# A fused attention and mixture-of-experts layer: GpSimd's indirect DMAs in groups that wait for TensorE

## The chip, the cores and the metric

The kernel runs on one core of a Trainium2 chip. The metric is the device time of one execution in microseconds (us); lower is better. It is given as the median of several runs.

## The reference

One transformer layer on x of 16 sequences x 128 tokens x 256 features (2048 tokens), in float32, with a context of the same shape:

```python
x = x + xattn(layernorm(x), ctx, ctx, pad_mask, subsq_mask, Wq, bq, Wk, bk, Wv, bv)   # 16 heads of 16
h = layernorm(x)
ys = geglu(h @ Ws1 + bs1) @ Ws2 + bs2                      # shared expert, hidden width 512
logits = (h @ Wr + br) / 1.5
top_val, top_idx = top_k(logits, 2); top_w = softmax(top_val)
yE = geglu(h @ We1[e] + be1[e]) @ We2[e] + be2[e]          # 12 experts, hidden width 768
x = x + ys + sum over the two chosen e of top_w * yE
```

`geglu(a|g)` is `a * gelu(g)`. The reference computes every expert for every token and weights with zeros; the kernel computes only the chosen ones, 128 token copies at a time.

## The kernel before, in words

Each engine has its own program and they meet at semaphores. TensorE multiplies float32r operands split in a high and a low part, so each product takes three matmuls.

**Attention.** The sequences go in eight pairs p = 0..7 (`each_pair`; `PAIRS` is 8). Pairs 1 to 4 are a loop, pairs 0, 5, 6 and 7 are written out. Each pair has four units n = 0..3 (a sequence and half of its heads). In unit n TensorE computes `scores` (L540, L545, then `scores_ready` +1, so it is 4p+n+1 after unit n), transposes the probabilities of the unit before (L557, `pt_ready`), multiplies them with the values (L569, `pv_done`), and every second unit transposes the output back (L578). Between these it works for the next pair: transposes and projections (L461, L484, L492), and the router of the pair before (L461, L509). ScalarE copies the transposes out of PSUM (L832 `probT`, L837 `outT`, which waits for `pv_done`) and takes exponentials (L841); VectorE finds maxima (L1090), subtracts them (L1096), divides and adds the residual. Pair 7 has no next pair, so its units have less in them.

**Routing.** VectorE chooses the two experts of each token in three batches of 8, 4 and 4 tiles of 128 tokens (`BATCHES`) and writes row numbers (`idx_top`, `rows_ready` +1 each). GpSimd then scatters the normalized tokens with `scatter(t)` (L1523 to L1527): two indirect DMAs of 128 rows x 1 KB for tile t, from SBUF (`xn2_all`) to DRAM (`rows_in`). In GpSimd's program these stand at four places:
- pair 6, behind its layernorm step for pair 5 (`rstd`, L1425 and L1427) and waits for `rows_ready` 1: tiles 0 to 3, 8 DMAs;
- pair 7: tiles 4 to 7, then, behind `rows_ready` 2, tiles 8 to 11, in all 16 DMAs;
- after `expert(0)`, behind `rows_ready` 3: tiles 12 to 15, 8 DMAs.

Then `load_up_bias(0)` (L1533, waits for `out_rows_ready`), `expert(1)` and so on. `expert(e)` splits the weights that were loaded to `stage1` and `stage2` into the ring: `convert` (L1433, L1437), the next load (L1492), `convert_down` (L1446, L1450), the next load (L1496). SyncE loads the first rows of a slot only when all 32 scatters have landed (`scattered`, L428).

**Feed forward.** TensorE goes through 8 tiles of the shared expert (`FRONT` = 8), 43 slots of routed tokens (`SLOTS`), and the other 8 tiles of the shared expert (`BACK` = 8; `B0` = 51 is the number of tiles before them). A tile is: up product (L657, `up_ready`), bias on VectorE (L1313), gelu on ScalarE (L899), gate on VectorE (L1318), transposes (L671, `ht_ready`), high part on ScalarE (L906), low part on VectorE (L1322), down product (L704, L708 for a slot, L706 to L708 for a shared tile, ending in L710 with `y_ready`). The next tile's tokens are transposed in L688 (`xt_ready`) and split in L916 and L1327. VectorE adds the result to `x_all` (L1340, shared tile) or writes `y_row` (L1337, slot); both add 1 to `y_done`, which is therefore B0+1 when the first back tile is done. SyncE stores the slots' results to DRAM (`rows_out`, L432).

**The end.** When `y_done` has reached FRONT + SLOTS and all stores of slots have landed, GpSimd gathers every token's two results with 32 indirect DMAs of 128 rows x 1 KB (L1601, two for each of 16 tiles). VectorE adds them (L1403, `combine(t)`): tiles 2(i-2) and 2(i-2)+1 after back tile i, for i = 2 to 7, and tiles 12 to 15 after the last back tile. SyncE stores each finished tile (L451).

Of the kernel before, what the change touches and what calls it, by code (L numbers as in the profile page):

```python
# [28 lines left out]
TILES = N // P  # L29
# [22 lines left out]
def build(nc, x_d, ctx_d, pad_d, sub_d, wq_d, wk_d, wv_d, bq_d, bk_d, bias_d, tab_d, ws1_d, ws2_d, w1_d,  # L52
# [177 lines left out]
    def sem(name):  # L230
# [11 lines left out]
    scores_ready, shifted, maxed, exp_done, pt_ready, pt_copied, pv_done, normed = map(sem, (  # L242
        "scores_ready", "shifted", "maxed", "exp_done", "pt_ready", "pt_copied", "pv_done", "normed"))
# [27 lines left out]
    y_ready, y_done, shared_bias_in, sel_down_ready = map(sem, (  # L271
        "y_ready", "y_done", "shared_bias_in", "sel_down_ready"))
# [70 lines left out]
    B0 = FRONT + SLOTS  # L343
# [6 lines left out]
    with block:  # L350
# [1071 lines left out]
        def _(gp):  # L1422
            def rstd(var_sem, out_sem, mv, ve_t, rs_t, q, step_sem):
                gp.wait_ge(var_sem, q + 1)
                pool.tensor_tensor(ve_t[:, :], mv[:, :, 1], eps[:, :], ALU.add).then_inc(step_sem, 1)  # L1425
                gp.wait_ge(step_sem, q + 1)
                pool.tensor_tensor(rs_t[:, :], ve_t[:, :], half[:, :], ALU.pow).then_inc(out_sem, 1)  # L1427

            def convert(src, hi_ap, lo_ap, count):

                n = src.shape[1]
                for c in range(0, n, PIECE):
                    last = pool.tensor_scalar(hi_ap[:, c:c + PIECE], src[:, c:c + PIECE], 1.0, 0.0, ALU.mult, ALU.add)  # L1433
                last.then_inc(conv_hi, 1)
                gp.wait_ge(conv_hi, count)
                for c in range(0, n, PIECE):
                    last = pool.tensor_tensor(lo_ap[:, c:c + PIECE], src[:, c:c + PIECE],  # L1437
                                              hi_ap[:, c:c + PIECE].bitcast(f32), ALU.subtract)
                return last

            def convert_down(src, both_ap, count):

                both = both_ap.rearrange("p (c h n) -> p c h n", h=2, n=D)
                raw = src.rearrange("p (c n) -> p c n", n=D)
                for c in range(0, raw.shape[1], 2):
                    last = pool.tensor_scalar(both[:, c:c + 2, 0, :], raw[:, c:c + 2, :], 1.0, 0.0, ALU.mult, ALU.add)  # L1446
                last.then_inc(conv_hi, 1)
                gp.wait_ge(conv_hi, count)
                for c in range(0, raw.shape[1], 2):
                    last = pool.tensor_tensor(both[:, c:c + 2, 1, :], raw[:, c:c + 2, :],  # L1450
                                              both[:, c:c + 2, 0, :].bitcast(f32), ALU.subtract)
                return last
# [6 lines left out]
            for c in range(KC):  # L1459
                n = H  # L1460
# [30 lines left out]
            def load_raw1(e):  # L1491
                gp.dma_start(stage1[:, :].rearrange("p (c n) -> p c n", c=KC),  # L1492
                             w1_d[e, :, :].rearrange("(c p) n -> p c n", p=P)).then_inc(raw1_in, 16)

            def load_raw2(e):
                gp.dma_start(stage2[:, :].rearrange("p (c n) -> p c n", n=D),  # L1496
                             w2_d[e, :, :].rearrange("(c p) n -> p c n", p=P)).then_inc(raw2_in, 16)
# [6 lines left out]
            def pair(p, par, first, last):  # L1504
                if not first:
                    rstd(ln2_var, ln2_rs, mv2, ve2, rs2, p - 1, pstep2)
                if not last and not (isinstance(p, int) and p + 2 >= PAIRS):
                    rstd(ln1_var, ln1_rs, mv1, ve1, rs1, p + 2, pstep)
                if isinstance(p, int) and p == PAIRS - 2:
                    gp.wait_ge(zero_out, 16 * FILLS)  # L1510
                    gp.wait_ge(xn2_saved, 16 * 4)
                    gp.wait_ge(rows_ready, 1)
                    for t in range(0, 4):
                        scatter(t)
                if last:
                    for t in range(4, 8):
                        scatter(t)
                    gp.wait_ge(xn2_saved, 16 * 6)
                    gp.wait_ge(rows_ready, 2)
                    for t in range(8, 12):  # L1520
                        scatter(t)

            def scatter(t):  # L1523
                for k in range(2):
                    gp.indirect_dma_start(
                        out=rows_in, out_offset=bass.IndirectOffsetOnAxis(ap=idx_top[:, k, t:t + 1], axis=0),
                        in_=xn2_all[:, t * D:(t + 1) * D], in_offset=None).then_inc(scattered, 16)  # L1527

            each_pair(gp, pair)
            rstd(ln2_var, ln2_rs, mv2, ve2, rs2, PAIRS - 1, pstep2)  # L1530

            def load_up_bias(e):
                gp.dma_start(up_bias[:, e % RING, :],  # L1533
                             bias_d[e, 0:2 * HR].partition_broadcast(P))\
                    .then_inc(up_bias_in if e else first_bias_in, 16)

            def expert(e):

                r = e % RING
                if e > 0:  # L1540
                    load_up_bias(e)
                gp.wait_ge(raw1_in, 16 * (e + 1))
                convert(stage1[:, :], ring[:, r, 0:W1R], ring[:, r, W1R:2 * W1R], 2 * e + 3).then_inc(pconv, 1)
                gp.wait_ge(pconv, e + 1)
                if e + 1 < E:
                    load_raw1(e + 1)
                else:
                    gp.dma_start(stage1[:, 0:W1S].rearrange("p (c n) -> p c n", c=KC),
                                 ws1_d.rearrange("(c p) n -> p c n", p=P)).then_inc(raw1_in, 16)
                gp.wait_ge(raw2_in, 16 * (e + 1))  # L1550
                if e > 0:
                    gp.wait_ge(up_bias_in, 16 * e)
                convert_down(stage2[:, :], ring[:, r, 2 * W1R:], 2 * e + 4)\
                    .then_inc(converted, 1)
                gp.wait_ge(converted, e + 2)
                if e + 1 < E:
                    load_raw2(e + 1)
                else:
                    gp.dma_start(stage2[:, 0:W2S].rearrange("p (c n) -> p c n", n=D),
                                 ws2_d.rearrange("(c p) n -> p c n", p=P)).then_inc(raw2_in, 16)  # L1560
# [3 lines left out]
            gp.wait_ge(normed, B)  # L1564
            gp.wait_ge(xb_free, PAIR_STEPS_END + 2)
            expert(0)

            gp.wait_ge(xn2_saved, 16 * PAIRS)
            gp.wait_ge(rows_ready, len(BATCHES))
            for t in range(12, TILES):  # L1570
                scatter(t)
            gp.wait_ge(tables_ready, 1)
            gp.wait_ge(out_rows_ready, 1)
            load_up_bias(0)
            expert(1)
            for e in range(2, E):
                if e == 2:
                    gp.wait_ge(y_done, FRONT)
                else:
                    done = gp.value_load(tab_cum[0:1, e - RING:e - RING + 1], min_val=1, max_val=SLOTS + FRONT)  # L1580
                    gp.wait_ge(y_done, done)
                    pool.tensor_tensor(ptick[:, :], half[:, 0:1], half[:, 0:1], ALU.add)
                expert(e)
# [13 lines left out]
            for par in range(2):  # L1597
                gp.wait_ge(y_out[par], 16 * ((SLOTS + 1 - par) // 2))
            for t in range(TILES):
                for k in range(2):  # L1600
                    gp.indirect_dma_start(  # L1601
                        out=gath[:, t, k, :], out_offset=None, in_=rows_out,
                        in_offset=bass.IndirectOffsetOnAxis(ap=idx_out[:, k, t:t + 1], axis=0))\
                        .then_inc(gathered[t], 16)
# [59 lines left out]
```

## Time and profile before

| | |
|---|---|
| median of 3 runs | 753.22 us (750.91 to 760.72) |
| the profiled execution's own time | 759.51 us |
| its span, first to last instruction | 757.7 us |
| mean granted TensorE clock | 0.920 of full |
| TensorE matmuls busy | 646.5 us (85%) |
| VectorE busy | 484.7 us (64%) |
| GpSimd busy | 347.5 us (46%) |
| ScalarE busy | 300.7 us (40%) |

Times are from the span's start. In the trace PE is TensorE, DVE is VectorE, ACT is ScalarE, POOL is GpSimd, SP is SyncE. A row of a timeline gives start, duration, engine, line, operation, what is written from what, how often; in brackets stands how long the engine had been idle before and what ended that. "remote" there is an end for which the trace has a semaphore update, but no instruction that had just finished; "issue" is an end without such an update at that moment. PEclk is the clock that TensorE was granted, of 2.4 GHz; its two levels are 2.4 and 1.2 GHz.

### The profile page before, as it was taken

To read this page: it belongs to the slowest core of one execution; us is meant where nothing else is said; L and a number is where in the kernel's file an instruction comes from. 1 tells how busy PE (TensorE), PEld (TensorE's weight loads), DVE (VectorE), ACT (ScalarE), POOL (GpSimd) and SP (SyncE) were. 2 spreads that over 40 slices of the span, in tenths; PEclk is the share of its full clock that TensorE was granted. 3 is DMA by queue.
4 is the path that set the end of the run, shared out by engine and by line. 5 is a ranking of instruction groups with operands and counts; after the bars stand their busy time and mean duration, and the time that the engine had idled before them with its cause. 6 is when DMAs were issued, how large, how long until landed. Compare 5 with 4: busy or idle time off the path is not lost.

```text
span 757.7 us, 14868 instructions
## 1 busy us (share of the span) xinstructions
PE 646.5 (85%) x4276; PEld 536.5 (71%) x4277; DVE 484.7 (64%) x1077; ACT 300.7 (40%) x685; POOL 347.5 (46%) x404
## 2 busy tenths in 40 slices
PE   7889989998968287699999999999999999993264
PEld 6778777877755265587878878787887878883163
DVE  7667767768734237976666767676666666762086
ACT  4445555554532042135434444444444444430021
POOL 3950000000120707796497489478974860027500
PEclk9989999999965668999999999999999999996687
DMA  9964522536010300553443544353545320113311
GB/s 294 402 218 163 210 107 101 208 140 251 24 47 1 117 8 17 177 181 114 153 166 119 193 148 167 123 193 133 194 129 177 121 78 28 35 42 119 90 42 56
DMA packets 48178, 100.07 MB, mean 132 GB/s; under 512 B 4624, under 2 KB 23824, under 8 KB 48144
## 3 DMA queue, kind: packets, MB, share of 16 engines
q1 hardware_dynamic: 36320, 51.06, 19.0%
q0 software_dynamic: 11120, 48.24, 19.0%
q10 hardware_dynamic: 704, 0.33, 0.2%
q8 instruction: 20, 0.33, 0.2%
q14 instruction: 14, 0.11, 0.0%
HBM read 58.19 MB, written 39.19 MB: 129 GB/s over the span
## 4 chain that ended last, share of the span: by engine, by line
PE 72%; DVE 10%; issue 7%; another core or an unknown queue 5%; ACT 5%; POOL 1%; DMA 1%; DVEq 0%; ACTq 0%; SPq 0%; POOLq 0%
PE ps_s L657 27%; PE ps_o L704 8%; PE ps_o L708 5%; PE ps_t L557 4%; PE ps_o L569 4%; PE ps_s L545 4%; PE ps_t L671 3%; PE ps_t L484 2%; ACT probT L832 2%; PE ps_x L484 2%; PE ps_s L540 2%; DVE x_all L1403 2%; PE ps_x L679 1%; PE ps_s L671 1%
## 5 line engine op out<-in xcount | busy, mean ns | idle before, releaser
L657 PE MATMUL ps_s<-ring,xTh 128*128 (+1 forms) x644 | 193.0, 422 | 13.2 <-issue 12.6
L657 PEld LDWEIGHTS ps_s<-ring,xTh 128*128 128x128 f32 x644 | 112.1, 192 | 31.4 <-issue 13.5
L1313 DVE TENSOR_TENSOR ag<-ps_s,up_bias 128x512 f32<-128x512 f32 x145 | 99.9, 689 | 26.3 <-remote 14.4
L657 PE MATMUL ps_s<-ring,xTl 128*128 (+1 forms) x322 | 101.6, 397 | 0.0
L1437 POOL TENSOR_TENSOR ring<-stage,ring 128x512 fp32r<-128x512 f32 x80 | 100.6, 1291 | 1.2
L1425 POOL TENSOR_TENSOR ve<-mv,eps 128x2 f32<-128x2 f32 x16 | 3.9, 247 | 207.2 <-DVE mv L1122 166.0
L704 PE MATMUL ps_o<-ring,hTh 128*128 x258 | 95.9, 409 | 1.0 <-DVE hTl L1322 1.0
L708 PE MATMUL ps_o<-ring,hTl 128*128 (+1 forms) x322 | 92.5, 287 | 0.0
L906 ACT ACTIVATE hTh<-ps_t 128x256 fp32r<-128x256 f32 x118 | 45.2, 384 | 109.8 <-PE ps_t L671 80.1
L899 ACT ACTIVATE ps_s<-ag 128x256 f32<-128x256 f32 x161 | 62.6, 389 | 48.8 <-DVE ag L1313 45.2
L1318 DVE TENSOR_TENSOR ag<-ag,ps_s 128x256 f32<-128x256 f32 x161 | 67.7, 421 | 20.2 <-ACT ps_s L899 2.1
L832 ACT ACTIVATE probT<-ps_t 128x512 f32<-128x512 f32 x64 | 38.2, 596 | 87.0 <-PE ps_t L557 83.3
L657 PEld LDWEIGHTS ps_s<-ring,xTl 128*128 128x128 f32 x322 | 61.3, 190 | 14.3
L1322 DVE TENSOR_TENSOR hTl<-ps_t,hTh 128x256 fp32r<-128x256 f32 x118 | 49.5, 420 | 26.3 <-ACT hTh L906 21.3
L708 PEld LDWEIGHTS ps_o<-ring,hTl 128*128 128x128 f32 x322 | 63.2, 196 | 0.0
L1601 POOL DMA_INDIRECT gath<-rows_out,idx_out x32 | 30.6, 957 | 67.1 <-DMA rows_out<-y_row 57.7
L704 PEld LDWEIGHTS ps_o<-ring,hTh 128*128 128x128 f32 x258 | 48.5, 188 | 11.0 <-issue 1.5
L1337 DVE TENSOR_TENSOR y_row<-ps_o,y_lo 128x256 f32<-128x256 f32 x43 | 18.3, 425 | 55.8 <-ACT y_lo L924 55.8
L671 PE MATMUL ps_t<-const,ag 128*128 128x128 f32 x236 | 46.7, 280 | 5.9 <-issue 5.8
L1450 POOL TENSOR_TENSOR ring<-stage,ring 128x512 fp32r<-128x512 f32 x40 | 50.6, 1292 | 1.2
L557 PE MATMUL ps_t<-const,prob 128*128 128x128 f32 x256 | 45.3, 304 | 6.6 <-ACT probT L832 5.2
L1433 POOL TENSOR_SCALAR ring<-stage 128x512 fp32r<-128x512 f32 x80 | 47.2, 618 | 4.7 <-DVE logits L1037 4.3
(253 smaller groups left out, 1275.1 us busy)
## 6 DMA issues: line engine op xcount, KB each, us to landing
rows_in<-y_row SPq DMA_DIRECT2D x8, 3328.0 KB, 11.2
stage<-in_w POOLq DMA_DIRECT2D x12, 1536.0 KB, 6.7
stage<-in_w POOLq DMA_DIRECT2D x12, 768.0 KB
up_bias<-in_bias POOLq DMA_DIRECT2D x12, 768.0 KB, 4.6
xrow<-rows_in SPq DMA_DIRECT2D x43, 128.0 KB, 2.3
rows_out<-y_row SPq DMA_DIRECT2D x43, 128.0 KB, 1.7
cbuf<-in_ctx SPq DMA_DIRECT2D x8, 256.0 KB, 3.2
xn_all<-xn2p SPq DMA_DIRECT2D x8, 256.0 KB
```

Of the source, the lines that this page charges most:

```text
L557: last = pe_.transpose(ps_t[:, 0, g * P:(g + 1) * P], prob[n % 2][:, jj, g, :], ident)
L657: last = pe_.matmul(ps_s[:, i, :], x[:, c, :], weights(place, off + c * full + i * 2 * D, 2 * D), start=n == 0, stop=n == 5)
L671: last = pe_.transpose(hid_bank[i][:, c * P:(c + 1) * P], ag[i][:, 0, c * P:(c + 1) * P], ident)
L704: pe_.matmul(ps_o[:, :], hTh[i][:, c, :], weights(place, a, 2 * D), start=first, stop=False)
L708: pe_.matmul(ps_o[:, 0:D], hTl[i][:, c, :], weights(place, a, D), start=False, stop=False)
L832: act.activation(probT[:, jj, :, :], ps_t[:, 0, :].rearrange("p (g t) -> p g t", g=4), ACT.Identity).then_inc(pt_copied, 1)
L899: act.activation(ps_s[:, i, D:2 * D], ag[i][:, 1, :], ACT.Gelu).then_inc(gelu_done[i], 1)
L1313: vec.tensor_tensor(ag[i][:, :, :].rearrange("p a n -> p (a n)"), ps_s[:, i, :], bias, ALU.add)\
L1318: vec.tensor_tensor(ag[i][:, 0, :], ag[i][:, 0, :], ps_s[:, i, D:2 * D], ALU.mult).then_inc(hid_done[i], 1)
L1322: vec.tensor_tensor(hTl[i][:, :, :], hid_bank[i].rearrange("p (c n) -> p c n", c=2), hTh[i][:, :, :].bitcast(f32), ALU.subtract).then_inc( ...
L1437: last = pool.tensor_tensor(lo_ap[:, c:c + PIECE], src[:, c:c + PIECE], hi_ap[:, c:c + PIECE].bitcast(f32), ALU.subtract)
L1450: last = pool.tensor_tensor(both[:, c:c + 2, 1, :], raw[:, c:c + 2, :], both[:, c:c + 2, 0, :].bitcast(f32), ALU.subtract)
```

## The change

In GpSimd's program the scatters and gathers get waits between them:
- pair 6: before tiles 0, 1, 2 and 3 a wait for the scores of unit 0, 1, 2 and 3 of that pair;
- pair 7: tiles 4 and 5 wait for the scores of unit 0, tiles 6 and 7 for those of unit 1, tiles 8 and 9 (beside their old waits) for those of unit 3;
- tiles 10 and 11 go out inside `expert(0)`, between the load for expert 1 that follows `convert` and `convert_down`;
- tiles 12 and 13 keep their place, tiles 14 and 15 wait for `y_done` 3;
- the gathers of tiles 4 and 5 wait for `y_done` B0+1, and so on to those of tiles 14 and 15, which wait for B0+6.

The number of DMAs and their sizes stay the same.

```diff
@@ pair() of gpsimd, p = PAIRS - 2, and the last pair
-                    for t in range(0, 4):
-                        scatter(t)
+                    for n in range(4):
+                        gp.wait_ge(scores_ready, 4 * p + n + 1)
+                        scatter(n)
                 if last:
-                    for t in range(4, 8):
-                        scatter(t)
+                    for n in range(2):
+                        gp.wait_ge(scores_ready, 4 * p + n + 1)
+                        scatter(4 + 2 * n)
+                        scatter(5 + 2 * n)
                     gp.wait_ge(xn2_saved, 16 * 6)
                     gp.wait_ge(rows_ready, 2)
-                    for t in range(8, 12):
+                    gp.wait_ge(scores_ready, 4 * p + 4)
+                    for t in (8, 9):
                         scatter(t)
@@ expert(e), after the load of stage1 for the next expert
+                if e == 0:
+                    for t in (10, 11):
+                        scatter(t)
                 gp.wait_ge(raw2_in, 16 * (e + 1))
@@ after expert(0)
-            for t in range(12, TILES):
+            for t in (12, 13):
+                scatter(t)
+            gp.wait_ge(y_done, 3)
+            for t in (14, 15):
                 scatter(t)
@@ the gathers
             for t in range(TILES):
+                if t % 2 == 0 and t >= 4:
+                    gp.wait_ge(y_done, B0 + t // 2 - 1)
                 for k in range(2):
```

## Rows read from the trace of the kernel before

**Rows 1.** The page, part 2: granted TensorE clock in 40 slices.

```profile
PEclk9989999999965668999999999999999999996687
```

**Rows 2.** The page, part 4: the chain that ended last, by engine.

```profile
PE 72%; DVE 10%; issue 7%; another core or an unknown queue 5%; ACT 5%; POOL 1%; DMA 1%; DVEq 0%; ACTq 0%; SPq 0%; POOLq 0%
```

**Rows 3.** Instructions by line: the scatters, then the gathers (ns min/median/max, starts in us).

```profile
L1525 POOL DMA_INDIRECT rows_in<-xn_all,idx_top x32: 956/960/1210, 205.2 to 318.5; - x32
...
L1601 POOL DMA_INDIRECT gath<-rows_out,idx_out x32: 942/946/1171, 675.7 to 714.9; - x32
```

**Rows 4.** Timeline around the first eight scatters (pair 6).

```profile
205.22 1.21 POOL L1525 DMA_INDIRECT rows_in<-xn_all,idx_top  x1 [0.20 <-issue]
...
208.91 0.60 ACT L832 ACTIVATE probT<-ps_t 128x512 f32<-128x512 f32 x1 [0.15 <-PE ps_t L557]
...
210.13 1.07 PE L569 MATMUL ps_o<-probT,v_sb 128*32 128x128 f32 x16
...
214.33 0.96 POOL L1525 DMA_INDIRECT rows_in<-xn_all,idx_top  x1 [0.30 <-issue]
216.90 0.60 ACT L837 ACTIVATE outT<-ps_o 128x512 f32<-128x512 f32 x1 [7.39 <-remote]
```

**Rows 5.** Timeline around the next sixteen scatters (pair 7).

```profile
245.44 1.17 POOL L1525 DMA_INDIRECT rows_in<-xn_all,idx_top  x1 [0.19 <-issue]
...
254.10 1.90 PE L569 MATMUL ps_o<-probT,v_sb 128*32 128x128 f32 x16 [3.16 <-ACT probT L832]
254.49 0.96 POOL L1525 DMA_INDIRECT rows_in<-xn_all,idx_top  x1 [0.30 <-issue]
...
264.61 0.96 POOL L1525 DMA_INDIRECT rows_in<-xn_all,idx_top  x1 [0.30 <-issue]
265.52 0.60 ACT L837 ACTIVATE outT<-ps_o 128x512 f32<-128x512 f32 x1 [11.47 <-remote]
```

**Rows 6.** Timeline of the gathers and the back tiles.

```profile
683.19 0.62 PE L657 MATMUL ps_s<-ring,xTl 128*128 128x512 f32 x2
...
685.10 0.42 DVE L1340 TENSOR_TENSOR x_all<-ps_o,x_all 128x256 f32<-128x256 f32 x1 [3.06 <-remote]
...
692.92 0.69 DVE L1313 TENSOR_TENSOR ag<-ps_s,up_bias 128x512 f32<-128x512 f32 x1 [4.98 <-remote]
...
694.85 0.95 POOL L1601 DMA_INDIRECT gath<-rows_out,idx_out  x1 [0.30 <-issue]
...
698.90 0.63 PE L671 MATMUL ps_t<-const,ag 128*128 128x128 f32 x2
...
712.10 2.08 PE L657 MATMUL ps_s<-ring,xTh 128*128 128x512 f32 x4 [12.57 <-issue]
...
721.07 0.42 DVE L1340 TENSOR_TENSOR x_all<-ps_o,x_all 128x256 f32<-128x256 f32 x1 [8.70 <-remote]
...
751.07 0.42 DVE L1340 TENSOR_TENSOR x_all<-ps_o,x_all 128x256 f32<-128x256 f32 x1 [2.71 <-PE ps_o L710]
```

**Rows 7.** TensorE timeline: starts of the mask products (L540) of four units.

```profile
191.09 0.60 PE L540 MATMUL ps_s<-mask_b,ident_b 128*128 128x512 bf16 x2
...
205.07 0.61 PE L540 MATMUL ps_s<-mask_b,ident_b 128*128 128x512 bf16 x2
...
218.46 1.06 PE L540 MATMUL ps_s<-mask_b,ident_b 128*128 128x512 bf16 x2
...
245.95 1.03 PE L540 MATMUL ps_s<-mask_b,ident_b 128*128 128x512 bf16 x2
```

**Rows 8.** Busy time by window: PE, PEld, DVE, ACT, POOL, PEclk, DMA share, GB/s.

```profile
217.50:244.30 26.80, 23.10 (x140) 17.71 (x142) 13.70 (x31) 9.09 (x15) 0.05 (x1) 0.56 0.00 1
...
724.90:751.10 26.20, 22.07 (x121) 18.85 (x121) 20.45 (x47) 6.72 (x19) 0.00 (x0) 0.89 0.12 41
```

**Rows 9.** GpSimd's timeline behind the last eight scatters.

```profile
322.07 1.15 POOL L1533 DMA_DIRECT2D up_bias<-in_bias  x2 [2.58 <-DVE idx_out L1253]
...
349.03 0.56 POOL L1533 DMA_DIRECT2D up_bias<-in_bias  x1 [6.62 <-DVE x_all L1340]
```

## The prediction

> **What bounds the kernel now.** I read the clock by slices first [rows 1]: it is near full nearly everywhere, and falls to 0.5 to 0.8 in two places, slices 12 to 16 (208 to 303 us) and the last four (682 us to the end). The chain of waits [rows 2] is TensorE's for 72%, but has 7% "issue" and 5% of an unknown releaser, together about 90 us of 757.7. The instructions by line [rows 3] show what those places have in common: the 32 scatters run between 205.2 and 319.5 us and the 32 gathers between 675.7 and 715.9 us. Each takes 0.96 us of GpSimd, and one starts every 1.26 us (the first scatter of pair 6 at 205.22, the eighth at 214.33 [rows 4]).
>
> The timeline says what happens in such a burst. In pair 6 TensorE ends its value product at 211.20, and ScalarE's copy, which waits for nothing else, starts at 216.90, marked "remote": the semaphore update is there, but 5.7 us after the matmul [rows 4]. The last scatter had ended at 215.29. In pair 7 the value product ends at 256.00 and the same copy starts at 265.52; the sixteenth scatter runs 264.61 to 265.57 [rows 5]. In the gathers an up product ends at 683.81 and VectorE's bias step for it starts at 692.92; TensorE starts its next up product only at 712.10, after 12.57 us of idleness; and the down product finished by 699.1 lets VectorE go at 721.07 [rows 6]. So my reading is: **TensorE's releases are held up while GpSimd issues indirect DMAs one after the other**, and they get through when it stops. At a burst's start it does no harm: ScalarE took the release of a product that ended 3.5 us into the first burst after 0.15 us [rows 4]. Releases 6 us in and later are the ones held.
>
> How soon after a burst's end they get through differs: 1.6 us in pair 6 (215.29 to 216.90), none in pair 7, 5.2 us in the gathers (715.9 to 721.07). I take 1.6 us and keep 0 and 5.2 as ends.
>
> **Pair 6.** GpSimd reaches tile 0 at 205.22 because of its layernorm step, when the scores of units 0 and 1 are long done; those of unit 2 begin at 205.07 [rows 7] and are done before tile 2's turn at 210.3. So three of the four waits pass at once, six DMAs go unbroken, to 212.8, and the last two wait for unit 3's scores. The held release then comes at 212.8 + 1.6 = 214.4 instead of 216.9: gain 2.5 us (ends 4.1 and 0). The wait needs TensorE to go on, and TensorE waits for nothing of GpSimd's there; behind it in GpSimd's queue stands the layernorm step of pair 6, some 25 us later. The last two DMAs are 2.5 us long, below the 3.5 us that did no harm: 0.
>
> **Pair 7.** The layernorm step again brings GpSimd there after the scores of unit 1 have begun, so tiles 4 to 7 are eight DMAs unbroken, 245.44 to 255.45 [rows 5]. Then it waits for unit 3's scores, which need the held release. That comes at 255.45 + 1.6 but not before the product ends at 256.00, so about 257.5 instead of 265.5: gain 8.0 us (ends 9.5 and 4.8). Tiles 8 and 9 follow as four DMAs of 5.0 us where there were none; a release in their last 1.5 us may be late: -0.5 us (0 to -5.0, the group's length).
>
> **Tiles 10 to 15.** Four DMAs (5.0 us) enter `expert(0)` ahead of the second conversion, so both the expert's weights and the last eight scatters are up to 5.0 us later. VectorE writes its tables during the last burst and GpSimd idles 2.58 us behind it until `out_rows_ready` [rows 9]; 2.4 us of delay are left, and GpSimd idles 6.62 us before expert 2 for `y_done` [rows 9], so the conversions absorb it. SyncE's first row loads wait for all scatters and come some 5 us later too, at about 327; their tokens are used beside the eighth front tile, which ends by 349 [rows 9]. `y_done` 3 has come when tiles 14 and 15 are reached. What remains is held releases in the front tiles: -1 us (0 to -5).
>
> **Gathers.** `y_done` B0+2 comes at 685.5 [rows 6] and B0+1 a tile before it, both before they are asked for. So 16 gathers go unbroken as now, to 695.8, and only the wait for B0+3 holds. Releases open at 695.8 + 1.6 = 697.4; TensorE's down product ends at about 699.5 anyway [rows 6], and its next input, split by ScalarE and VectorE after the release, is ready by then. So `y_done` B0+3 comes at about 700 instead of 721.5. From there to the last back tile it takes 30.0 us now (721.07 to 751.07, five tiles of 6.0 us [rows 6], clock 0.89 [rows 8]). I add 2 us because the clock will be low for longer at its start, and four groups of gathers, 5.0 us each beside a tile of 6.0 us. A release in a group's last 1.5 us may be late; 0.75 us each, 3 us. The last tile then ends at 700 + 30 + 5 = 735 instead of 751.5: gain 16.5 us. Best end: without these 5 us 21.5, and 3.3 more if the clock is 1 and not 0.89 over the 30 us: 24.8. Worst: the release 5.2 us late instead of 1.6 and each group holding its tile for its whole 5.0 us: 16.5 + 3 - 3.6 - 20 = -4. The last gathers wait for B0+6, two tiles (12 us) before they are needed, and take 5 us: they don't set the end.
>
> **Sum.** 2.5 + 8.0 - 0.5 - 1 + 16.5 = 25.5 us against the profiled execution's 759.51: 734.0. That execution lies 6.3 us above the median of 753.22, and the runs spread over 9.8 us. If that spread is in the held releases, it goes with them and 734.0 stands; if it lies elsewhere, 727.7. I take the middle, 731, in round numbers **730 us**, and move all prices below by the same -4.
>
> **The clock.** After the first stall TensorE ran 26.8 us at a mean of 0.56, busy for 23.1 of them [rows 8]; before it, at full clock, two units took 14.0 us [rows 7], and after it the three from 218.46 to 245.95 took 27.5 instead of 21.0. So a stall costs up to 6.5 us more behind its end. I give nothing of that back, since six DMAs in a row still leave a stall of about 3 us at the same place. The Trainium skill's TensorE: Matmul & The Clock Gate ("HAM oscillation") says that idle gaps drop the clock, so that they are paid twice; by that rule the shorter gap would give back up to these 6.5 us as well. The trace agrees that the low level follows the gap; whether a gap half as long spares it, no row shows.
>
> **Rivals.**
> - **A, the stalls go with their aftermath.** All best ends: 4.1 + 6.5 (clock) + 9.5 + 24.8 = 44.9 us, so 714.6, moved 711. For it: a release 3.5 us into a burst was on time. Against: pieces of 6, 8 and 16 DMAs stay unbroken. 0.15.
> - **B, paced gathers are a burst all the same.** A group is 5.0 us of a 6.0 us tile, so GpSimd hardly pauses, and what holds releases may not clear in 1 us. Then the gather term is 0 and 9.0 us are left: 750.5, moved 747. For it: 5.2 us passed after the last gather before anything came through. Against: each group starts only after a release has come. 0.13.
> - **C, slower: each gather group meets its tile's releases.** The group is now let go by `y_done`, just as the next tile's up products start, so every tile from B0+4 on has its releases inside a group. The trace has one release 9.1 us late (692.92 for the product of 683.81 [rows 6]). With 9.1 us on each of five tiles the last ends at 700 + 5 x 15.1 = 775.5, 24 us later than now; less 9 us of the scatters, 774.5, moved 771. It decides from tiles of (751.5 + 9 - 700) / 5 = 12.1 us on. Against: the start of a burst did no harm. 0.06.
> - **D, the releases aren't held by GpSimd's DMAs.** Most waits pass at once, the total stays: 753. For it: the last eight scatters, 309 to 319 us, sit beside no such drop of the clock [rows 1]. Against: both other scatter bursts and the gathers do. 0.06.
>
> My forecast has 0.60, with its own range of 720 to 741. The range for 8 times in 10 reaches to A and B: 710 to 748. About 2%, 15 us, can be told from no change, so below 738.2 counts as faster: most of my case and A, 0.78; the rest of it, B and D, 0.16; C, 0.06.
>
> **What would show it.** In pair 6 six scatters, a gap, two; in pair 7 eight, a gap, four. ScalarE's `outT` copies start near 214 and 257 us. In the gathers 16 without a break to 695.8, then four at a time, VectorE's third back tile (L1340) near 700, then tiles of 6 to 7 us, no "remote" or "issue" idleness over 3 us. Conversions from expert 2 on unchanged against `y_done`. I am wrong if the held releases come as late as before though GpSimd has stopped, if GpSimd's four-DMA groups each show one, or if the scatters in pair 6 have gaps where I let them pass.

## The result, and the profile after

The kernel after takes 730.00 us (median of 6 runs, 727.31 to 732.60), the kernel before 756.34 us (median of 6, 750.35 to 760.72): ratio 0.966 (0.959 to 0.972), 26.3 us faster. The forecast was 730. The profiled execution took 727.32 us. A ratio here and below leaves out executions more than 1.5% above the fastest of the same kernel, so that it can differ a little from the quotient of the two medians.

The page after: the span, the busy times, the clock by slices and the chain's shares.

```profile
span 725.4 us, 14869 instructions
...
PE 639.4 (88%) x4276; PEld 532.0 (73%) x4277; DVE 485.3 (67%) x1077; ACT 301.3 (42%) x685; POOL 347.7 (48%) x404
...
PEclk9989999999988678899999999999999999999697
...
PE 75%; DVE 11%; issue 7%; ACT 4%; another core or an unknown queue 1%; DMA 1%; POOL 1%; SPq 0%; DVEq 0%; ACTq 0%; POOLq 0%
```

Against [rows 1 and 2]: "an unknown releaser" went from 5% to 1% of the chain, the clock dips are shallower, and the engines are as busy as before. So the time came out of waiting.

The timeline after, scatters of pairs 6 and 7 with ScalarE's copies of the value products between them:

```profile
204.96 1.15 POOL L1529 DMA_INDIRECT rows_in<-xn_all,idx_top  x1 [0.26 <-issue]
...
211.50 0.96 POOL L1529 DMA_INDIRECT rows_in<-xn_all,idx_top  x1 [0.30 <-issue]
213.76 0.60 ACT L837 ACTIVATE outT<-ps_o 128x512 f32<-128x512 f32 x1 [4.56 <-remote]
...
218.57 0.96 POOL L1529 DMA_INDIRECT rows_in<-xn_all,idx_top  x1 [6.11 <-PE ps_s L545]
...
238.76 1.16 POOL L1529 DMA_INDIRECT rows_in<-xn_all,idx_top  x1 [0.20 <-issue]
...
247.42 0.60 ACT L837 ACTIVATE outT<-ps_o 128x512 f32<-128x512 f32 x1 [4.17 <-remote]
247.81 0.96 POOL L1529 DMA_INDIRECT rows_in<-xn_all,idx_top  x1 [0.30 <-issue]
...
252.77 0.96 POOL L1529 DMA_INDIRECT rows_in<-xn_all,idx_top  x1 [3.99 <-PE ps_s L545]
```

Six scatters, a gap, two; then eight, a gap, four: the groups are those forecast. The first late release comes 8.80 us after the first scatter (11.68 in [rows 4]), the second 8.66 us after it (20.08 in [rows 5]). The second comes before the eighth scatter starts, so a burst does not have to end for a release to get through.

The timeline after, gathers and back tiles:

```profile
661.87 1.05 POOL L1613 DMA_INDIRECT gath<-rows_out,idx_out  x1 [57.57 <-DMA rows_out<-y_row]
...
680.74 0.95 POOL L1613 DMA_INDIRECT gath<-rows_out,idx_out  x1 [0.30 <-issue]
682.55 0.38 ACT L906 ACTIVATE hTh<-ps_t 128x256 fp32r<-128x256 f32 x1 [10.20 <-remote]
...
683.49 0.55 PE L706 MATMUL ps_o<-ring,hTh 128*128 128x256 f32 x1 [11.72 <-issue]
...
684.76 0.38 ACT L916 ACTIVATE xTh<-ps_x 128x256 fp32r<-128x256 f32 x1 [1.55 <-remote]
...
686.64 0.42 DVE L1340 TENSOR_TENSOR x_all<-ps_o,x_all 128x256 f32<-128x256 f32 x1 [0.37 <-PE ps_o L710]
...
687.33 0.94 POOL L1613 DMA_INDIRECT gath<-rows_out,idx_out  x1 [5.65 <-DVE x_all L1340]
...
693.79 0.94 POOL L1613 DMA_INDIRECT gath<-rows_out,idx_out  x1 [1.76 <-DVE x_all L1340]
...
698.49 0.28 PE L710 MATMUL ps_o<-bias_tab,sel_s 128*128 128x256 f32 x1
...
699.52 0.42 DVE L1340 TENSOR_TENSOR x_all<-ps_o,x_all 128x256 f32<-128x256 f32 x1 [0.62 <-PE ps_o L710]
...
718.78 0.42 DVE L1340 TENSOR_TENSOR x_all<-ps_o,x_all 128x256 f32<-128x256 f32 x1 [3.25 <-PE ps_o L710]
```

Sixteen gathers still go unbroken (661.87 to 681.69) and still hold TensorE: it stands idle for 11.72 us before 683.49, because ScalarE's `hTh` is released only at 682.55, 0.9 us after the burst. Then four groups of four follow, 1.7 us apart, with a back tile every 6.4 us, and not one "remote" among them. Yet their releases are not on time: TensorE's product ends at 698.77 and VectorE takes it at 699.52, 0.75 us later and 1.05 us after the group's last gather, and it is 0.75 to 0.78 us in each of the four groups.

Stage by stage, gain of the profiled executions (757.7 against 725.4 us of span) beside the forecast:

| stretch | before | after | gain | forecast |
|---|---|---|---|---|
| first scatter to late `outT`, pair 6 | 205.22 to 216.90 | 204.96 to 213.76 | 2.9 | 2.5 |
| to pair 7's first scatter | to 245.44 | to 238.76 | 3.5 | 0 |
| to late `outT`, pair 7 | to 265.52 | to 247.42 | 11.4 | 8.0 |
| to the first front tile's end (L1340) | to 297.93 | to 280.21 | -0.4 | -0.5 |
| to the first gather | to 675.74 | to 661.87 | -3.8 | -1 |
| first gather to the span's end | to 757.7 | to 725.4 | 18.4 | 16.5 |
| up to the first scatter | 205.22 | 204.96 | 0.3 | 0 |
| sum | | | 32.3 | 25.5 |

On the medians it is 26.3.

### The profile page after: what moved, and what is told of

The parts are those of the page before. It is cut to its first block, busy times and chain, and to the rows that moved or that the text cites. A ratio compares the mean times of both kernels' runs of the same rounds, so it can differ in the third digit from the quotient of the medians.

```text
span 725.4 us, 14869 instructions
## 1 busy us (share of the span) xinstructions
PE 639.4 (88%) x4276; PEld 532.0 (73%) x4277; DVE 485.3 (67%) x1077; ACT 301.3 (42%) x685; POOL 347.7 (48%) x404
## 4 chain that ended last, share of the span: by engine, by line
PE 75%; DVE 11%; issue 7%; ACT 4%; another core or an unknown queue 1%; DMA 1%; POOL 1%; SPq 0%; DVEq 0%; ACTq 0%; POOLq 0%
PE ps_s L657 29%; PE ps_o L704 8%; PE ps_o L708 5%; PE ps_t L557 4%; PE ps_o L569 4%; PE ps_s L545 4%; PE ps_t L671 3%; PE ps_x L484 2%; PE ps_t L484 2%; DVE x_all L1403 2%; ACT probT L832 2%; PE ps_s L540 2%; PE ps_o L706 2%; PE ps_o L710 1%; PE ps_x L679 1%
## 5 line engine op out<-in xcount | busy, mean ns | idle before, releaser
L1337 DVE TENSOR_TENSOR y_row<-ps_o,y_lo 128x256 f32<-128x256 f32 x43 | 18.3, 425 | 55.7 <-ACT y_lo L924 55.7
L706 PE MATMUL ps_o<-ring,hTh 128*128 128x256 f32 x64 | 21.7, 339 | 31.3 <-issue 27.9
```

## The experiments

Theory H: while GpSimd issues indirect DMAs without a pause, TensorE's releases to other engines are held, and a pause lets them through. Rival D: the late releases have another cause, and the waits gain by ordering alone. Beside these, each part of the change was priced alone.

The runs fell into four sittings, on chips 8, 12, 1 and 9, each with its own runs of the kernel before. That kernel took 754 and 759 us (medians) on chips 12 and 9, much as in the result, but 697 us on chips 8 and 1. Each verdict below is against the kernel before of the same sitting.

**Sitting 1 (chip 8, kernel before 697.10 us, 25 runs, one of them of 1535.75 us): the parts alone.**

`gathers_only` is the kernel before with the waits of the gathers:

```diff
                 for t in range(TILES):
+                    if t % 2 == 0 and t >= 4:
+                        gp.wait_ge(y_done, B0 + t // 2 - 1)
```

> The kernel before with only the waits between the gathers. Theory (TensorE's releases are held while GpSimd issues indirect DMAs without a break): the scatter bursts keep their held releases, ScalarE's outT copies near 216.9 and 265 us, and the gather stage is shorter by 16 to 19 us, as in the changed kernel: some 18 us under the time of before, about 738. Rival (the gathers gain only because the scatters left the engines in another state): under 8 us gained.

Measured 697.34 us (10 runs), ratio 1.001 (0.997 to 1.004).

`scatters_only` is the kernel after without these two lines:

> The changed kernel without the waits between the gathers. Theory: the scatter part is worth what the profiles differ by at the first gather, 13.9 us, so about 742; the gather stage keeps its three long waits and its 82 us from first gather to end. Rival (the two parts overlap in what they save): under 8 us gained.

Measured 700.71 us (10), ratio 1.005 (1.003 to 1.008).

`landing_waits` leaves the scatters alone and has the gathers pause every four DMAs for something that has nothing to do with TensorE, the landing of the last ones:

```diff
                 for t in range(TILES):
+                    if t % 2 == 0 and t >= 2:
+                        gp.wait_ge(gathered[t - 1], 32)
```

> The kernel before, where each group of four gathers waits until the group before has landed, with no wait for TensorE at all. Theory (a pause of GpSimd is what lets releases through, whoever it waits for): pauses of about 1 to 2 us after every 4 gathers, no wait of over 3 us for an unknown releaser in the back tiles, gain 18 to 28 us (more than gathers_only, as no 16 go unbroken), about 730. Rival (the wait for TensorE is what matters, since it starts each group when no release is due): held releases as before in most groups, gain under 8 us.

Measured 710.22 us (4), ratio 1.022 (1.014 to 1.030).

`ten_behind` is the kernel after with tiles 10 and 11 moved back out of `expert(0)`:

```diff
-                if e == 0:
-                    for t in (10, 11):
-                        scatter(t)
...
-            for t in (12, 13):
+            for t in (10, 11, 12, 13):
                 scatter(t)
```

> The changed kernel with the scatters of tiles 10 and 11 moved out of expert(0), to just before those of tiles 12 and 13. Theory (they push GpSimd's second conversion onto VectorE's short row number operations, which then take 1 us each, and cost most of the 4.2 us that the front tiles lost against before): front tiles 2 to 4 us shorter, 727 or less. Rival (the loss comes from scatters beside the front tiles, wherever they stand): twelve scatters nearly in a row there, no gain or a loss of up to 3 us.

Measured 699.63 us (10), ratio 1.002 (0.997 to 1.007).

None of the times expected could be met, since here there was nothing to win; what `ten_behind` expected of the front tiles is taken up below. The timeline of `gathers_only`, whose scatters are those of the kernel before, shows ScalarE's copies in pairs 6 and 7 beside the first and last of pair 7's sixteen scatters, then one product and its use in the back tiles:

```profile
210.28 0.60 ACT L837 ACTIVATE outT<-ps_o 128x512 f32<-128x512 f32 x1 [1.87 <-PE ps_o L569]
...
231.69 1.17 POOL L1525 DMA_INDIRECT rows_in<-xn_all,idx_top  x1 [0.19 <-issue]
...
237.95 0.60 ACT L837 ACTIVATE outT<-ps_o 128x512 f32<-128x512 f32 x1 [1.76 <-PE ps_o L569]
...
248.30 0.60 ACT L837 ACTIVATE outT<-ps_o 128x512 f32<-128x512 f32 x1 [1.19 <-PE ps_o L569]
...
251.06 0.96 POOL L1525 DMA_INDIRECT rows_in<-xn_all,idx_top  x1 [0.31 <-issue]
...
668.03 0.28 PE L710 MATMUL ps_o<-bias_tab,sel_s 128*128 128x256 f32 x1
...
668.36 0.42 DVE L1340 TENSOR_TENSOR x_all<-ps_o,x_all 128x256 f32<-128x256 f32 x1
```

Sixteen scatters without a break, 0.96 us each, every 1.26 us, as in [rows 5]. Two copies start 6.3 and 16.6 us into them, each 0.07 us after TensorE's product. In the back tiles VectorE takes the product 0.05 us after its end (668.31), with gathers going out all the while. No wait of TensorE, ScalarE or VectorE around the scatters or gathers ends "remote", in this or any other kernel profiled in such a sitting, and the back tiles come every 5.7 us. So the bursts are the same in both kinds of sitting, and what differs is whether they hold releases. The difference of the two kernels before is 57 to 63 us. From the end of the first front tile to the first gather both kinds take 377.8 us (266.94 to 644.74 here, 297.93 to 675.74 before); all of the difference lies in the stages with the bursts. So it is the price of the held releases with their aftermath, and about what there is to win by removing them.

**Sitting 2 (chip 12, kernel before 753.97 us, 7 runs): both kernels once more,** to see whether result and trace belong together.

> The kernel before, unchanged, profiled on the chip of this call. In the last call its median was 697 us, not 756, and the scatter bursts of gathers_only and landing_waits held no release. Theory now: held releases belong to some chips or cores and not to others, and they are the whole difference of about 58 us. So either the median is near 697 and the profile shows no wait of over 3 us for an unknown releaser in the bursts, or it is near 756 and shows those of the first profile. Rival (the 697 us came from something else, say a faster clock in the routed tiles): near 697 with held releases still in the bursts, and the time gained evenly over the span.

> The changed kernel, unchanged, beside it. Theory: where before takes about 697 us the waits have nothing to remove and cost what the front tiles lose, 0 to 5 us: 697 to 703. Where before takes about 756 it is near 730 again. Rival (the waits gain by something beside held releases): over 5 us faster than before on a chip without them.

The kernel after took 730.24 us (4), ratio 0.969 (0.960 to 0.977). The profiled execution of the kernel before took 760.49 us and has its late copies back:

```profile
216.32 0.60 ACT L837 ACTIVATE outT<-ps_o 128x512 f32<-128x512 f32 x1 [7.37 <-remote]
...
264.29 0.60 ACT L837 ACTIVATE outT<-ps_o 128x512 f32<-128x512 f32 x1 [13.60 <-issue]
...
717.69 0.69 DVE L1313 TENSOR_TENSOR ag<-ps_s,up_bias 128x512 f32<-128x512 f32 x1 [14.93 <-remote]
```

The gain goes with the held releases: where they are there it is 24 and 26 us, where they aren't its parts are worth nothing. (The kernel after as a whole was never timed there.)

**Sitting 3 (chip 1, kernel before 696.76 us, 19 runs).** `paced` applies the finding that six or eight DMAs are still too long a group. Pairs 6 and 7 scatter in groups of four behind the scores of units 1 and 3, tiles 10 to 15 go out behind `expert(0)` (two waits for `y_done` 3 stand between them, both long met), and every group of four gathers waits for the latest tile. Against the kernel after, in part:

```diff
-                    for n in range(4):
-                        gp.wait_ge(scores_ready, 4 * p + n + 1)
-                        scatter(n)
+                    for n in range(2):
+                        gp.wait_ge(scores_ready, 4 * p + 2 + 2 * n)
+                        scatter(2 * n)
+                        scatter(2 * n + 1)
...
-                    gp.wait_ge(scores_ready, 4 * p + 4)
+                    gp.wait_ge(pv_done, 2 * UNITS - 2)
                     for t in (8, 9):
...
-                if t % 2 == 0 and t >= 4:
-                    gp.wait_ge(y_done, B0 + t // 2 - 1)
+                if t % 2 == 0 and t >= 2:
+                    gp.wait_ge(y_done, B0 + t // 2)
```

> The changed kernel with groups of four from the start: gathers of tiles 2 and 3 wait for the first back tile, those of 14 and 15 for the seventh; in pairs 6 and 7 four scatters, then a wait for unit 3's scores, four more, and the last four of pair 7 wait for the value products; tiles 10 and 11 after expert(0). Theory (no group of four holds a release): where before takes about 756 the outT waits and the 10 us waits of the first 16 gathers go too, 15 to 25 us under the changed kernel, 705 to 715. Rival (four in a row already hold when the group is let go by TensorE): 725 or more. Where before takes about 697: 695 to 705.

Measured 699.94 us (10), ratio 1.003 (1.000 to 1.006).

`gathers_only` and `landing_waits` were run again:

> The same kernel as gathers_only, for a chip on which before takes about 756 us. Theory (holds of releases in each unbroken burst, the two parts add up): outT copies late by 6 and 9 us or more in the scatter bursts as in before, gather stage (first gather to end) 63 to 66 us instead of 82, so 735 to 740. Rival (the parts aren't independent): gather stage over 72 us. If before takes about 697 here: no difference, as in the first call.

> The same kernel as landing_waits, for a chip on which before takes about 756 us: each group of four gathers waits for the landing of the group before, not for TensorE. Theory (GpSimd's pause lets releases through): pauses of 2 to 3 us, no wait for an unknown releaser over 3 us in the back tiles; the gather stage is as short as in gathers_only_2 or up to 5 us shorter. Rival (the wait must be tied to TensorE's progress): such waits in most groups, stage over 72 us. If before takes about 697 here: some 13 us slower than before, as in the first call.

They took 698.94 us (10), ratio 1.000 (0.996 to 1.004), and 710.38 us (4), ratio 1.016 (1.010 to 1.021).

`direct_pool` was to tell an indirect DMA from a plain one, by issuing the gathers of the kernel before as plain DMAs of the same size:

```diff
-                    gp.indirect_dma_start(
-                        out=gath[:, t, k, :], out_offset=None, in_=rows_out,
-                        in_offset=bass.IndirectOffsetOnAxis(ap=idx_out[:, k, t:t + 1], axis=0))\
+                    gp.dma_start(gath[:, t, k, :], rows_out[(2 * t + k) * P:(2 * t + k + 1) * P, :])\
```

> The kernel before with the 32 gathers as plain GpSimd DMAs of the same size (128 rows of 1 KB each, from fixed rows, so the rows that are combined are not the chosen ones). The burst stays unbroken. Theory (what holds releases is GpSimd's row-by-row work for indirect DMAs): no wait over 3 us for an unknown releaser in the back tiles, stage under 62 us. Rival (any unbroken row of GpSimd DMAs holds them, or the data's traffic does): held releases as in before. Where before takes about 697: no statement.

Measured 696.32 us (1 run), in a sitting where nothing is held anyway: it says nothing of the mechanism.

**Sitting 4 (chip 9, kernel before 759.49 us, 7 runs): the two that tell most, where releases are held.**

> The same kernel as paced, for a chip on which before takes about 756 us. Theory (four indirect DMAs in a row hold no release, six and more do): no wait over 3 us for an unknown releaser in pair 7 and in the back tiles, 15 to 25 us under the changed kernel's 730, so 705 to 715. Rival (a group of four let go by TensorE's progress holds them as well, only shorter): 722 or more, with such waits of 3 to 5 us left in most groups. If before takes about 697 here: no gain over before, as in the last call.

Measured 715.81 us (4), ratio 0.944 (0.936 to 0.952): 43.7 us below the kernel before, and with its 715.8 against 730 in the other sittings better than the kernel after. Its timeline, the first and the last of ScalarE's four `outT` copies of pairs 6 and 7, then gathers and back tiles:

```profile
211.81 0.60 ACT L837 ACTIVATE outT<-ps_o 128x512 f32<-128x512 f32 x1 [1.83 <-PE ps_o L569]
...
258.63 0.60 ACT L837 ACTIVATE outT<-ps_o 128x512 f32<-128x512 f32 x1 [2.37 <-PE ps_o L569]
...
654.74 1.07 POOL L1614 DMA_INDIRECT gath<-rows_out,idx_out  x1 [57.64 <-DMA rows_out<-y_row]
...
664.90 0.42 DVE L1340 TENSOR_TENSOR x_all<-ps_o,x_all 128x256 f32<-128x256 f32 x1 [3.89 <-remote]
...
665.60 0.95 POOL L1614 DMA_INDIRECT gath<-rows_out,idx_out  x1 [1.00 <-issue]
...
671.34 0.38 ACT L906 ACTIVATE hTh<-ps_t 128x256 fp32r<-128x256 f32 x1 [4.65 <-remote]
...
672.29 0.55 PE L706 MATMUL ps_o<-ring,hTh 128*128 128x256 f32 x1 [7.66 <-DVE hTl L1322]
```

The four copies start 0.07 to 0.40 us after their products. But the expectation of no wait over 3 us for an unknown releaser was missed. Beside the last eight scatters of pair 7, and behind the twelve that go out in a row beside the front tiles, releases come up to 1.7 us late. In the gathers the wait in the middle of the first eight is met at once, and four more follow after a pause of only 1.00 us. There VectorE's wait of 3.89 us ends "remote", and so do two of ScalarE's `hTh`, of 5.76 and 4.65 us. The transposes for the second of these had ended at 663.02, 8.3 us before, and TensorE stands idle for 7.66 us before 672.29. The release came 1.0 us after the last of the twelve gathers (670.30). A pause of 1.00 us, then, is too short. The first gather comes 7.1 us earlier than in the kernel after, and from there to the span's end (713.8 us) it takes 59.1 us instead of 63.5.

> The same kernel as landing_waits, for a chip on which before takes about 756 us: its groups of four gathers are separated by the wait for their own landing, with no tie to TensorE; the scatters are those of before. Theory (GpSimd's pause of 2 to 3 us lets the releases through): no wait over 3 us for an unknown releaser in the back tiles, gather stage 60 to 66 us instead of 82, about 738. Rival (the tie to TensorE's progress is what helps): such waits remain in most groups, stage over 72 us. If before takes about 697 here: some 13 us slower than before.

Measured 734.09 us (4), ratio 0.971 (0.962 to 0.980). Its scatters are those of the kernel before and hold about as much as there; its gathers pause. The timeline:

```profile
218.55 0.60 ACT L837 ACTIVATE outT<-ps_o 128x512 f32<-128x512 f32 x1 [7.37 <-remote]
...
252.29 0.60 ACT L837 ACTIVATE outT<-ps_o 128x512 f32<-128x512 f32 x1 [4.17 <-remote]
...
266.58 0.60 ACT L832 ACTIVATE probT<-ps_t 128x512 f32<-128x512 f32 x1 [12.26 <-remote]
...
670.30 1.07 POOL L1603 DMA_INDIRECT gath<-rows_out,idx_out  x1 [57.59 <-DMA rows_out<-y_row]
...
678.10 0.94 POOL L1603 DMA_INDIRECT gath<-rows_out,idx_out  x1 [2.96 <-DMA gath<-rows_out,idx_out]
...
723.52 0.95 POOL L1603 DMA_INDIRECT gath<-rows_out,idx_out  x1 [0.30 <-issue]
```

Within one execution the unbroken scatters hold (waits of 7.37 and 12.26 us) and the paced gathers hardly do: no wait in the back tiles ends "remote", those that end "issue" are of at most 2.4 us before the last tile, and VectorE takes seven of the eight products of the back tiles within 0.1 us of their end, the eighth (683.88) 1.4 us after, though the pauses of 2 to 3 us are tied only to landings. From the first gather to the span's end (729.6 us) it takes 59.3 us, against 82.0 before. That is the run that decides for H in the gathers: the waits need not name TensorE, a pause is enough. Its price is elsewhere: its last gather starts at 723.52, when TensorE's last tile is long added (717.95), and so it sets the end. Where nothing is held, only this price is left, the 13 us of sittings 1 and 3.

**What the scatters' part is worth.** Up to the first gather `landing_waits_3` is the program of the kernel before once more, so it shows what these stages do without any change. Five executions in which releases are held, side by side (lateness is from the end of TensorE's product to the copy's start):

| | scatters | first `outT` copy, pair 6, late by | from it to pair 7's first scatter | PEclk there | pair 7's first scatter to first front tile | first gather at |
|---|---|---|---|---|---|---|
| before | unbroken | 5.70 | 28.5 | 0.56 | 52.5 | 675.74 |
| `before_again` | unbroken | 5.69 | 26.5 | 0.63 | 56.1 | 676.65 |
| `landing_waits_3` | unbroken | 5.68 | 25.1 | 0.81 | 49.2 | 670.30 |
| after | 6+2, 8+4 | 2.87 | 25.0 | 0.81 | 41.5 | 661.87 |
| `changed_again` | 6+2, 8+4 | 2.90 | 22.9 | 0.85 | 40.9 | 661.87 |

The same unbroken scatters bring the first gather anywhere from 670.30 to 676.65. Of the 13.9 us that the profiled executions differ by there, 5.4 are thus seen without any wait between scatters, and 8.4 remain against `landing_waits_3`. The clock behind pair 6's stall is 0.56, 0.63 or 0.81 after a stall of the same length, so the 0.81 of the kernel after can't be put down to its shorter stall.

**The front tiles, from sitting 1.** The expectation of `ten_behind` was front tiles 2 to 4 us shorter. The forecast had -1 us between the first front tile and the gathers, and it was -3.8. The profile after puts this into one tile, 12.0 us (287.50 to 299.53) instead of 7.8. VectorE's row-number chain stands in it. First the kernel before, then the kernel after, VectorE's two last steps of that chain:

```profile
309.18 0.17 DVE L1268 TENSOR_SCALAR tiles_e<-cnt_s 128x12 f32<-128x12 int32 x1
309.39 0.18 DVE L1269 TENSOR_TENSOR_SCAN cum_e<-ones_e,tiles_e 128x12 f32<-128x12 f32 x1
```

```profile
291.14 3.71 POOL L1450 TENSOR_TENSOR ring<-stage,ring 128x512 fp32r<-128x512 f32 x3
...
292.54 1.11 DVE L1268 TENSOR_SCALAR tiles_e<-cnt_s 128x12 f32<-128x12 int32 x1
293.69 1.20 DVE L1269 TENSOR_TENSOR_SCAN cum_e<-ones_e,tiles_e 128x12 f32<-128x12 f32 x1
```

`ten_behind` against `scatters_only` tests it with nothing held. First `scatters_only`, then `ten_behind`, VectorE and GpSimd's `convert_down`:

```profile
284.64 3.73 POOL L1450 TENSOR_TENSOR ring<-stage,ring 128x512 fp32r<-128x512 f32 x3
...
284.70 1.25 DVE L1268 TENSOR_SCALAR tiles_e<-cnt_s 128x12 f32<-128x12 int32 x1
...
285.98 1.20 DVE L1269 TENSOR_TENSOR_SCAN cum_e<-ones_e,tiles_e 128x12 f32<-128x12 f32 x1
```

```profile
275.85 3.75 POOL L1450 TENSOR_TENSOR ring<-stage,ring 128x512 fp32r<-128x512 f32 x3
...
280.92 0.17 DVE L1268 TENSOR_SCALAR tiles_e<-cnt_s 128x12 f32<-128x12 int32 x1
281.12 0.18 DVE L1269 TENSOR_TENSOR_SCAN cum_e<-ones_e,tiles_e 128x12 f32<-128x12 f32 x1
```

With the four scatters in `expert(0)` the conversion lies on VectorE's chain, and steps of 0.17 us take 1.2 us, just one of the three GpSimd instructions (3.73 / 3 = 1.24). Without them it is over in time, and the tile takes 6.5 us instead of 9.8; all eight front tiles are 3.1 us shorter, as expected, though the medians (699.63 and 700.71 us) are too close to show it. The Trainium skill's SBUF — State Buffer ("SBUF: two separate sides") says that VectorE, in its two-port modes or with two inputs in SBUF, and GpSimd take a shared port pair as an exclusive lock for a whole instruction. These rows agree: the small step waits for about one whole instruction.

## Why the prediction came out

**Pair 6: right.** The release came 1.3 us after the sixth scatter's end (212.46), and I had 1.6. The gain was 2.9 us for a forecast of 2.5. That the waits of tiles 0 to 2 pass at once was right too.

**Pair 7: the sign right, the step wrong.** The term "255.45 + 1.6 but not before the product ends at 256.00" gave a release 12.1 us after the first scatter, let through by the end of the eight. It came 8.66 us after, during the burst, and 11.4 us were gained for 8.0. The pause had no part in that: `landing_waits_3`, with sixteen scatters unbroken, has the same copy 8.66 us after its first scatter (243.63), 2.10 us late as in the kernel after. In both the product ended 6.6 us after the first scatter (245.32 in the kernel after), where [rows 5] have 10.6: TensorE was further on when GpSimd began, and in the kernel before an earlier release was held as well, that for `probT` at 253.45, 2.95 us behind its transposes, which the forecast passed over. What the shorter groups do spare comes behind this copy. In `landing_waits_3` the next release is held for 8.7 us (266.58), in the kernel after none is, and from the copy to the first front tile it takes 40.5 us there and 32.8 here: 7.7 us.

**The clock: a term put at nothing that measured 3.5 us, and why stays open.** I gave back nothing between the two bursts "since six DMAs in a row still leave a stall of about 3 us". They do, and the clock behind it was higher in the profiled execution than in that of the kernel before. The window of the kernel after (busy times of PE, PEld, DVE, ACT, POOL, then PEclk), against 0.56 in [rows 8]:

```profile
213.80:238.70 24.90, 20.63 (x175) 16.54 (x176) 13.79 (x32) 10.45 (x16) 2.83 (x4) 0.81 0.03 12
```

The stretch from copy to first scatter, with the same work in it, is 3.5 us shorter. But `landing_waits_3` has the long stall (5.68 us late) and behind it the same clock, 0.81, and the same 25.1 us, while `before_again` has 0.63 and 26.5 us. So the forecast was wrong to take 0.56 as what follows the long stall, and no run shows that the shorter one gives time back. The forecast drew on the Trainium skill's TensorE: Matmul & The Clock Gate ("HAM oscillation") for idle gaps that are paid twice; that a shorter gap is paid for less behind it, these executions leave open. The 6.5 us for a stall's aftermath was too small besides, as it set the three units behind the stall against units of another make-up: with nothing held, at full clock, the same three take 18.3 us (`gathers_only`, mask products at 211.42 to 229.68) and not 21.0, so that the low clock of [rows 8] cost 9.2 us behind the stall.

**Front tiles: right sign, wrong reason.** The price of 1 us stood for "held releases in the front tiles". The row of one tile shows 4.2 us, 2.5 of them VectorE's row-number steps behind GpSimd's shifted conversion (6.3 us where they took 3.8). I had followed the conversion to `y_done` and the ring, where it is indeed absorbed, but not asked what runs beside it at its new place.

**Gathers: right.** The third back tile ended 24.8 us after the first gather (forecast 24.3), the paced tiles took 6.4 us each for a forecast of 6.0 and 0.75, and the low clock behind the stall cost less than the 2 us set for it. 18.4 us for 16.5. The 0.75 us for a release in a group's last 1.5 us is what the trace has in every group (0.75 to 0.78 us), and it is about what a tile takes more there (6.4 us) than in `gathers_only` (5.7).

**The level.** The spread between the profiled execution and the median was taken to go by half with the held releases. The profiled executions differ by 32.3 us of span, the medians by 26.3. The terms of the trace were 6.8 us short, and moving all prices by -4 made up for most of it. That part of the hit is luck. Both profiled executions of the kernel before (759.51 and 760.49 us) lie at the top of its 750 to 761 us, and `landing_waits_3` shows the same scatters 5.4 us cheaper; that the lower ones of the kernel before owe their time to this is likely, but none was profiled.

**The rivals.** A falls: the pieces of 6, 8 and 16 held on, and the higher clock isn't shown to come of the shorter stall. B and C name something that is there, but small: in the four paced groups each tile's last release is 0.75 us late, the tiles take 6.4 us, and C needed 12.1. D falls by `landing_waits_3`, but with an addition that no case of the forecast had: the hold is there in some sittings only. Where it isn't, the parts of the change are worth 0 (gathers) and cost 0.5% (scatters).

**What stays open.** Why a burst holds TensorE's releases, why one gets through in the middle of it, and why releases are held in some sittings alone. The two kinds differ in the chip and also in how many kernels shared a sitting (four beside the kernel before in 1 and 3, two in 2 and 4), so the two can't be told apart. Whether plain DMAs hold as well wasn't tried where anything is held, so it isn't shown whether the issuing by GpSimd or the traffic of the DMAs does it. And the split of the gain, 14 us up to the first gather and 18.4 from there on, rests on comparing two traces: the parts alone were timed only where there was nothing to win. `landing_waits_3` confirms the second part (its 59.3 us against 82.0), and leaves 8.4 us of the first.

## What to carry to other kernels

If a wait ends "remote" or "issue" with its matmul long done, look for a row of GpSimd's indirect DMAs beside it, and break it into groups of at most four with some 2 us of pause. Here pauses of 1.7 us left releases 0.75 us late, and one of 1.00 us left one of 8.3 us. What the pause waits for matters little, so tie it to something that comes early and never to the last landings. Then look at what the shifted GpSimd work now lies beside, VectorE's small steps above all. And before pricing such a change, time the kernel before in more than one sitting: here its time was 697 or 756 us, and the whole gain hangs on which. Before explaining a stretch by the change, look for the same stretch in another execution with the same program up to there: here it took away 5.4 of 13.9 us, and the explanation of the clock.

## What was unexpected of the hardware

The same program with the same cadence of DMAs holds TensorE's releases in some sittings, from 0.75 us (the paced groups after) to some 22 us (the down product finished by 699.1 and used at 721.07 [rows 6]), and shows no such wait in others: 754 to 759 against 697 us. `paced`, the best of all kernels where releases are held (715.8 us), is 0.3% above the kernel before where they aren't (699.94 us, ratio 1.003).

A held release is not bound to the burst's end. In the kernel after one came during a burst (247.42), as in `landing_waits_3` (252.29), others 0.9 and 3.1 us behind its last gather (682.55 and 684.76, for 681.69). After each paced group of four the release came 1.03 to 1.07 us behind the last gather.
